# A state-space layer with an expert layer on one core: the residual x is added by accumulating transfers into DRAM

## What is computed

```python
# x: (4, 1024, 1024), ctx: (4, 1024, 512), everything float32
def xattn(ctx, z):                       # a selective state-space layer
    x = einsum('bld,ed->bel', ctx, in_proj_w)
    x = silu(causal_conv4(x) + conv_b)
    dt_low, Bm, Cm = split(einsum('bdl,ed->bel', x, x_proj_w))
    dt = softplus(dt_proj_w @ dt_low + dt_proj_b)
    # per channel d and state n, along l:
    #   state = state * exp(dt * A) + (dt * x) * B ;  y = sum_n state * C
    return swap((y + D * x) * silu(z))
def ffn(x):                              # expert choice, 16 experts, one shared weight
    S = softmax(x @ router_w + router_b)
    G, idx = top_k(S.T, 256)             # 256 tokens of 4096 for each expert
    y[idx] += G * (x[idx] @ expert_w + expert_b)
    return y
x = x + tanh(g_xattn) * xattn(ctx, layernorm(x))   # this sum is called x2 below
x = x + tanh(g_ffn) * ffn(layernorm(x))
```

## Time and profile before

| | us |
|---|---|
| median of 3 runs | 2072.36 |
| lowest, highest run | 2070.16, 2072.4 |
| the profiled execution | 2071.91 |
| its span in the trace | 2069.8 |
| busy: DVE, POOL, PE, ACT | 1888.9, 1754.8, 1641.9, 1455.0 |
| of the span: DVE, POOL | 91%, 85% |
| mean granted TensorE clock | 0.891 |

### The profile page before, as it was taken

One profiled execution on the slowest core, in us unless ns is written; L12 is line 12 of the kernel. 1 busy time (PEld: TensorE's weight loads), 2 busy tenths in 40 slices (PEclk: granted clock), 3 DMA queues, 4 the chain that ended last, 5 costly groups with the idle time before them and its releaser, 6 DMA issues.

```text
span 2069.8 us, 23420 instructions
## 1 busy us (share of the span) xinstructions
PE 1641.9 (79%) x7572; PEld 1077.2 (52%) x7572; DVE 1888.9 (91%) x1974; ACT 1455.0 (70%) x2222; POOL 1754.8 (85%) x767
## 2 busy tenths in 40 slices
PE   8566666679888988888888988888888878788793
PEld 3334445555555555555555555555555555556341
DVE  5989899999999899999999899999999999994667
ACT  5878778786788677886888778876788677864000
POOL 0879999998999999998999999999999999996000
PEclk9778788799999999999999989999999988988996
DMA  7613161044745384345635374445535463437079
GB/s 261 243 47 123 50 237 68 22 158 149 261 133 170 107 297 151 105 162 201 223 118 180 119 287 130 142 141 215 200 106 158 170 244 112 125 96 282 6 303 387
DMA packets 138426, 346.10 MB, mean 167 GB/s; under 512 B 15170, under 2 KB 17730, under 8 KB 129346
## 3 DMA queue, kind: packets, MB, share of 16 engines
q1 hardware_dynamic: 138306, 344.61, 47.8%
HBM read 298.94 MB, written 45.61 MB: 166 GB/s over the span
## 4 chain that ended last, share of the span: by engine, by line
POOL 27%; PE 23%; DVE 17%; issue 16%; ACT 12%; DMA 5%; SPq 0%; DVEq 0%; POOLq 0%; ACTq 0%
POOL states L1468 16%; DVE states L1191 10%; POOL states L1456 9%; PE pY L656 6%; PE pM L750 4%; ACT pDec L919 4%; PE pA L621 3%; DVE states L1176 2%; PE pA L630 2%; ACT L903 1%; DMA bbc<-bc_scratch 1%; DVE u L1164 1%; POOL dtub L1447 1%; PE pY L652 1%; ACT L1109 1%
## 5 line engine op out<-in xcount | busy, mean ns | idle before, releaser
L1468 POOL TENSOR_TENSOR states<-states,cbc 128x2048 f32<-128x2048 f32 x255 | 1156.4, 4537 | 31.3 <-DVE states L1191 20.8
L919 ACT ACTIVATE pDec<-steps,an 128x512 f32<-128x512 f32 x1024 | 683.8, 686 | 348.5 <-DVE states L1191 343.8
L656 PE MATMUL pY<-con,states 128*128 128x128 f32 x4096 | 587.9, 306 | 189.0 <-POOL states L1468 189.0
L656 PEld LDWEIGHTS pY<-con,states 128*128 128x128 f32 x4096 | 541.9, 160 | 307.0 <-POOL states L1468 246.8
L1191 DVE TENSOR_TENSOR_SCAN states<-pDec,carry,states 128x512 f32<-128x512 f32 x512 | 626.2, 1266 | 24.2 <-ACT pDec L919 24.0
L1191 DVE TENSOR_TENSOR_SCAN states<-pDec,states 128x512 f32<-128x512 f32 x512 | 595.1, 1206 | 37.0 <-ACT pDec L919 36.8
L1456 POOL TENSOR_TENSOR states<-dtub,bbc 128x1024 f32<-128x1024 f32 x192 | 454.6, 2367 | 52.9 <-PE pY L656 42.6
L750 PE MATMUL pM<-wk,xfT 128*128 128x512 f32 x816 | 415.9, 625 | 0.0
L1176 DVE TENSOR_TENSOR states<-pU,bbc 128x1024 f32<-128x1024 f32 x320 | 385.6, 1205 | 8.2 <-DMA bbc<-bc_scratch 6.5
L621 PE MATMUL pA<-ctx_sb,winb 128*128 128x512 f32 x448 | 223.5, 645 | 54.0 <-issue 31.3
L750 PEld LDWEIGHTS pM<-wk,xfT 128*128 128x128 f32 x816 | 145.0, 204 | 78.3 <-issue 77.8
(11 more groups left out here) (232 smaller groups left out, 1461.8 us busy)
## 6 DMA issues: line engine op xcount, KB each, us to landing
wk<-in_expert_w SPq DMA_DIRECT2D x408, 256.0 KB, 4.3
cbc<-bc_scratch SPq DMA_DIRECT2D x32, 1024.0 KB, 9.5
bbc<-bc_scratch SPq DMA_DIRECT2D x31, 1024.0 KB, 7.4
sz<-in_x SPq DMA_DIRECT2D x32, 512.0 KB, 6.0
xt<-in_x SPq DMA_DIRECT2D x15, 1024.0 KB, 5.6
winb<-in_winT SPq DMA_DIRECT2D x58, 256.0 KB, 2.6
x_scratch<-xt SPq DMA_DIRECT2D x14, 1024.0 KB, 6.5
xr<-x_scratch SPq DMA_DIRECT2D x28, 512.0 KB, 4.1
```

The source lines that it names most:

```text
L656: mm = pe.matmul(pY[:, eT(t)], states[g % NST][:, i, eT(t)], ident, start=False, stop=(q == QG - 1 and i == QN - 1 and t == TT - 1), is_tr ...
L919: nc.scalar.activation(pDec[bank_of(h, k)][:], dt[e % 2], ACT.Exp, scale=an[:, k:k + 1]).then_inc(s_dec, 1)
L1468: nc.gpsimd.tensor_tensor(st, st, cbc[:, QW * q:QW * (q + 1), :], ALU.mult).then_inc(s_hc, 1)
```

## The change

In the seven halves 0 to 6, `y_out` multiplies `pY` by the gate straight into `xt`, and `add_x` is gone. SP copies x of the half from DRAM to `x2_scratch` in slot 10 (`copy_x`, 2 MB, one transfer), and POOL issues two transfers of 1 MB that add `xt` to it there (`add_to_x`, at the slots where SP stored). PE's first group of a block waits for `s_y`. `y_out` of blocks 0 and 4 waits until the transfer before has landed. Group 31 of each half (block 3, the last) is made by DVE and no more by POOL. Half 7 keeps `add_x` and its loads of x.

At the end, PE and ACT no more run the leftover slots but a short list of their own; the softmax of half 7 is made in two parts (tiles 0 to 2, then tile 3), tile 3's logits in another bank; and `NSLOT` is 10, the tenth pair in `pairs[1]`; the masks move to `unread`, and the search's work tiles all fit into `pairs[0]`.

```diff
-POOL_GROUPS = [g for g in range(NG) if g % QG in (1, 4, 7)]
+POOL_GROUPS = [g for g in range(NG) if g % QG in (1, 4, 7) and g != 3 * QG + 7]
-NSLOT = 9
+NSLOT = 10
@@ SP
-            def store_x2(h, part):
-                if h < NC - 1:
-                    wait(sp, s_x2, n(h, E, (part + 1) * (E // 2)))
-                    sp.dma_start(x2_dram[h, :, :, part * 512:(part + 1) * 512], xt[:]).then_inc(s_x2w, 16)
+            def copy_x(h):
+                sp.dma_start(x2_dram[h], x[h].rearrange("(t p) d -> p t d", p=P)).then_inc(s_xpre, 16)
...
             def load_x(h, part):
-                if h == 0 and part == 0:
-                    sp.wait_ge(s_rows, 5 * 2)
+                if h < LAST:
+                    return
...
-                for i, k in at(STX_SLOT, g, h):
-                    store_x2(k, i)
+                if g == 10 and h < LAST:
+                    copy_x(h)
@@ PE, sum_states
-                    wait(pe, s_x2, n(h, E, e))
+                    if h == LAST and e:
+                        pe.wait_ge(s_x2, e)
+                    else:
+                        wait(pe, s_y, n(h, E, e))
@@ PE, the end
-            half(NC, REST)
+            turn_gate(LAST, E - 1, n(NC, HALO * E, 0), n(NC, 1, 0))
+            turn_xf(LATE, 5, n(NC, E, 0), n(LATE, TT, 2))
+            for g in range(NG - 4, NG):
+                sum_states(LAST, g)
             turn_end(LATE, 6)
...
             for j in range(TT):
+                pe.wait_ge(s_stol, 1 if j < TT - 1 else 2)
                 mm = pe.transpose(pY[:, eT(j)], S_tok[:, j, :, :].rearrange("p c s -> p (c s)"), ident)
@@ ACT, the end
-            half(NC, REST)
-            norm_x2(LAST, 0)
+            row_mean(LATE, TT - 1)
+            row_variance(LATE, TT - 1)
+            gate_out(LAST, E - 1)
+            xfT_out(LATE, 5)
+            norm_x2(LATE, TT - 1)
             xfT_late(6)
             xfT_late(7)
+            norm_x2(LAST, 0)
             norm_x2(LAST, 1)
...
-            logits_end(LAST)
-            router_exp(LAST)
-            scores(LAST)
+            for part in range(2):
+                softmax_last(part)
@@ DVE, y_out
-                nc.vector.tensor_tensor(pY[:], pY[:], szT[(e + 1) % 2][:], ALU.mult).then_inc(s_y, 1)
+                if h == LAST:
+                    nc.vector.tensor_tensor(pY[:], pY[:], szT[(e + 1) % 2][:], ALU.mult).then_inc(s_y, 1)
+                    return
+                part, i = divmod(e, E // 2)
+                if i == 0:
+                    wait(dve, s_x2w, n(h, 32, 16 * part))
...
+                nc.vector.tensor_tensor(xt[:, :, eT(i)], pY[:].rearrange("p (t d) -> p t d", t=TT), gate, ALU.mult).then_inc(s_y, 1)
@@ POOL
+            def add_to_x(h, part):
+                pool.wait_ge(s_xpre, n(h, 16, 16))
+                pool.wait_ge(s_y, n(h, E, (part + 1) * (E // 2)))
+                nc.gpsimd.dma_start(x2_dram[h, :, :, part * 512:(part + 1) * 512], xt[:], accum_op=ALU.add).then_inc(s_x2w, 16)
...
+                for part, k in at(STX_SLOT, g, h):
+                    if k < LAST:
+                        add_to_x(k, part)
```

77 lines of the change are left out of this document (51 added, 26 removed).

## The result

| | before | after |
|---|---|---|
| median of 9 runs each | 2073.34 us | 2068.06 us |
| lowest to highest | 2070.16 to 2075.48 | 2066.14 to 2071.76 |
| profiled execution, its span | 2069.8 | 2068.1 |

The ratio is 0.9977, with a 95% interval from 0.9969 to 0.9986. The change makes the kernel faster, as forecast, but by 5 us and not by 26. The medians in this text are of executions in the fast state; one execution of the kernel with plain stores, 2128.55 us at a granted clock of 0.78, is left out.

What follows compares the result with a forecast made beforehand. DVE and POOL, each 96% busy, were taken to bound the loop together, with POOL held by PE's buffers. 2071.9 - 18 (loop) - 8 (end) = 2046 us; range 2038 to 2058 at 52%, 2029 to 2074 for 8 in 10.

Steps and rivals of the forecast that it cites:

- The add, -32.5 us off DVE: Loop, DVE: 56 adds of x, 0.58 us each, go; with group 31's +9.0, DVE's sum is -23.5 us.
- Group 31: Block 3 of each half: 8 products of 1.13 us come to DVE, +9.0 us; 19.0 us leave POOL.
- The transfers, 1.5 us each on POOL: Loop, POOL: issuing 14 accumulating transfers costs 21 us, bounds 7 to 63; the issue alone stops nobody at once.
- POOL's sum of +2 us: Loop: POOL's 21 us of transfers against the 19.0 us of group 31; bounds -12 to +44.
- PE let go sooner: First product of 56 blocks starts 3 us earlier; most of PE's 54.7 us and much of POOL's 26.7 us of waits go.
- Three quarters, -18 us: Loop: three quarters of DVE's 23.5 us counts as time, as POOL's waits fall; bounds 0 and -28.
- The end, -8 us: After the loop: earlier PE start 4.2, softmax 1.4 and ring 2.5 us together; bounds -4 and -10.
- the first two terms: The end: PE's last gapless stretch starts 4.2 us sooner, at 1881.6; the two-part softmax saves about 1.4 us.
- the ring: The end, combination of tiles: a tenth pair (1.05 MB) is loaded during the search, saving 2.5 us.
- The gain turns into a wait for ACT: Rival, loop: ACT's bursts set the pace and a lighter DVE only waits longer; end alone gains, 2064 us; 7%.
- POOL as the bound: Rival, loop: transfers of 4.5 us add 44 us to POOL, 2064 us; 15% together with crowded transfers, 2062 us.
- The accumulates did not land late: Rival, blocks 0 and 4: DVE's gate product waits for late landings; at 23 us to land, 2102 us; 12%.

## Why the prediction was wrong, step by step

- **The add, -32.5 us off DVE.** Right as work (DVE's busy time over the whole span fell by 22.6 us, with group 31's 9.0 in it; forecast 23.5), wrong as time. Five of each half's eight adds stood in the shadow of an ACT burst, a sixth about half in it. The step that failed is the one that took DVE's sum as what the loop can lose, "for the loop to lose 23.5 us, POOL [...] must lose that much of its waits". It looked for what would hold DVE back in POOL alone. The other one stands in the earlier trace rows, 48.7 us of DVE for ACT in 54 waits, but it was read as a total, not by place. The timeline of ACT at slots 5, 13, 21, 29 or 37 would have shown the burst behind the scan at which the add stood. The place of the earlier trace rows would not have shown it well: it is block 5's add, in slot 44, where the burst begins at 906.36, ahead of that scan.
- **Group 31.** DVE's +9.0 cost nearly nothing in the changed kernel, as block 3's shadow took it in. The 19 us off POOL bought nothing either: they are not in the chain of slots 37 to 40. Alone it was +1.0 us.
- **The transfers, 1.5 us each on POOL.** 1.60 measured. POOL's sum of +2 us was right: its busy time over the span grew by 3. But it counts by place. At slot 37 of an even half the transfer and what comes with it cost the block 3.1, of which idle work of the same length makes 1.7; "its issue alone stops nobody at once" is the sentence that failed, since the whole queue behind it was late.
- **PE let go sooner.** The wait of 54.7 us went, to 10.6, as forecast, and PE's wait for POOL grew by 28.9. So "with them much of POOL's 26.7 us" was wrong (32.7 now): POOL waited for PE at other places. Of its 47.5 us of waits, which were to fall, 51.5 are left (32.7 and 18.8).
- **"Three quarters, -18 us"** is the term that came out wrong, in its sign too: the loop became 6.8 us longer in the profiled execution, and 3 in the medians of the two parts (2.2 and 1.0).
- **The loop by halves**, after less before, from half 0 to 7: +1.0, -1.1, +4.4, -1.9, +2.7, -2.1, +3.6, -0.1, which with 0.2 of the start is the 6.8 of that execution. Half 0 is no measure (2.7 us between two executions of the same loop). In an odd half DVE's adds of blocks 6 and 7 are gone; in an even one block 5 costs 3.1, blocks 6 and 7 give back 1.2, and block 2 costs 1.1 more: DVE's wait for ACT at slot 22 grew there from 1.0 to 2.4 us, for a reason that I have not followed.
- **The end, -8 us.** -8.2 alone and -8.4 in the trace, and its terms by their places. The last stretch of PE without a gap was to begin at 1881.6; it begins at 1888.63, and less the loop's 6.8 that is 1881.8. The scores' last turn ends at 1916.95, less the loop's part 1910.2, where it ended at 1915.92: 5.7 us for the first two terms, forecast at 5.6, which leaves 2.7 for the ring, forecast at 2.5.

```profile
1888.63 1.97 PE L710 MATMUL pDec<-con,xr 128*128 128x128 f32 x8 [2.75 <-ACT xr L970]
...
1915.22 0.87 PE L868 MATMUL pY<-con,S_tok 128*128 128x128 f32 x3 [0.37 <-ACT S_tok L1038]
...
1916.47 0.48 PE L868 MATMUL pY<-con,S_tok 128*128 128x128 f32 x1 [0.38 <-ACT S_tok L1038]
```

- **The rivals.** "The gain turns into a wait for ACT" had 7% and 2064 us. It was the truth in blocks 0 to 4 of the odd halves. POOL as the bound (15%) holds in one block of the even halves, where it lost to the loop what the odd halves gained. The accumulates did not land late: 12 us were estimated, 19 allowed, and it was

```profile
L1537 POOL DMA_DIRECT2D x_scratch<-xt x14: 1213/1275/1419, 202.2 to 1689.3; - x14
...
DMA to landing us min/median/max: 8.3/8.8/11.9
```

What stays open: what paces the even halves in blocks 0 to 4, where a kernel with sooner bursts was no faster in sum; what makes the half of block 5's 3.1 us that idle work of the transfer's length does not; and why moving group 41 costs the odd halves 2.8 us in block 6.
